# Routed experts placed in the slots of the second attention, and causal masks of 64 columns

## The chip, the cores and the metric

One core of a Trainium2 chip runs the whole program in one launch. The metric is the device time of that core in microseconds; the median of three runs of the kernel before is 3800.89 (3798.13 to 3801.47). 

## The reference

Two layers on x of 16 x 512 x 128 (f32): each adds an attention-like part and a feed-forward part of the normalised x to x. Only layer 1 is touched here.

```python
xn = layernorm(x)
x = x + causal_attention_twice(xn) + routed_experts(xn)
# attention: q, k, v = xn @ Wqkv.T + b   (16 heads of 8), causal softmax -> ctx
#   q2 = conv1d(ctx, 3 taps); ctx2 = causal softmax of q2 with the same k, v; out = ctx2 @ out_w.T + b
# experts (32 of them, each of 128 slots, top 8 of 32 per token):
oh = one_hot(flat_e); pos = (cumsum(oh, 0) * oh).sum(-1) - 1
buf = zeros(E, 128, H).at[flat_e, pos].set(flat_x, mode='drop')
gate, up = split(einsum('ech,efh->ecf', buf, gate_up_proj))
eo = einsum('ecf,ehf->ech', silu(gate) * up, down_proj)
out = sum over the 8 chosen of weight * eo[expert, pos]     # dropped where pos >= 128
```

The attention has two passes over the same keys and values for each of 16 batches, so 32 passes. An expert takes the first 128 tokens that chose it.

## The kernel before

The program runs in stages, each with instruction lists written out by hand for all five engines and its own semaphores, which are cleared after it: `learn` (a memory trained chunk by chunk), `attend0`, `mixture` (dense experts of layer 0, which also leaves the table of normalised rows with expert weights, the sum so far, and `chosen`, a 0/1 flag for each token and expert), then `routed` (L1989) and `layer1` (L2262).

`routed` works through 32 experts in 8 groups of 4 (Q = 4), in loops. For a group, `indices` finds the token of each slot: four matmuls with an upper triangle give running counts in each of 64 tiles of tokens (L2100), one more the counts of earlier tiles (L2104), DVE makes one-hot rows for the tile of each slot (L2208 to L2214), matmuls select the tile's counts (L2108, L2110), and DVE compares and sums to a row index (L2216 to L2225). `through` passes the group: POOL gathers 128 rows per expert by an indirect DMA (L2163), TensorE transposes them (L2116), multiplies by the gate and up weights (L2122), ACT and DVE gate, TensorE transposes (L2126) and multiplies by the down weights (L2130), DVE scales by the token's share (L2244), and POOL adds each expert's rows into the sum in memory by an indirect DMA that accumulates (L2175). Adds follow one another, each waiting for the last to land, since two experts may hold one token.

`layer1` uses the class `Attention` (L964). A turn is one pass over one batch; there are 32, firsts and seconds mixed (batch b's second comes at least three turns after its first), plus turns -2 and -1 that only prepare and turn 32 that only ends. From turn 3 on, odd turns are seconds, and so is turn 30. A turn has 16 slots: four groups g of four heads, and four key tiles t of 128. In slot (g, t), `tensor_scores` (L1164) makes transposed scores of keys of tile t against queries from tile t on: width 512, 384, 256, 128. In the same slot `tensor_maxima` (L1135) makes the scores of the next turn's batch for the row maxima, of the same widths. ACT takes the exponentials (L1261), DVE the maxima (L1303), and `tensor_values` (L1192) multiplies the probabilities of the slot before by the values, in f32 (L1203). In tiles 0 and 1 (wide slots) the heads come in two units, the second after the first; in tiles 2 and 3 (narrow slots) all four heads go together. f32 operands of the scores are split into three bf16 parts, laid into partitions in groups of 8 (PITCH): six are used (PARTS), rows 62 and 63 of each half carry the shift by the maximum, and the other rows are zero. The two halves of 64 partitions hold two heads and run side by side.

PSUM banks are handed out by two rings (L941): `m` of two double banks (maxima, shift, context, values, output) which DVE frees, and `s` of three banks (exponentials, projections, convolution, whole transposes) which ACT frees. `plan` (L1053) lists the jobs of both in the order in which TensorE issues them; a job waits until the job two (m) or three (s) before it is freed. Extra jobs sit at fixed slots: query and key projections of a first at slots 0 and 4, values at 8, convolution of a second in two halves at 4 and 8, the whole transposes at slot 3, context transposes at slots 1 and 9, output at slot 5 of the turn after a second. ACT, DVE and TensorE follow the same order.

POOL splits q and k of turn p + 2 into parts once ACT has written them (`pool_parts`, L1093), SP copies the parts into the rows of the query and key buffers (`sync_rows`, L1119), and the maxima of the next turn but one wait for that. The causal mask is added by matmuls on top: for each tile a pair of halves n = 0, 1 picks (`pick`) rows of `qmask` or `kmask` with 0 or -1e30. For the maxima their widths are 128 and 64 columns (L1155), for the scores 64 and 128 (L1188), two halves of partitions each:

```python
for n in range(2):
    for half in range(2):
        rows = slice(half * HALF, (half + 1) * HALF)
        last = nc.tensor.matmul(outs[half][:, k0:k0 + HALF + n * HALF], self.pick[n][rows, :], self.kmask[n][rows, :], start=False, stop=n == 1)
```

## Time and profile before

| what | value |
|---|---|
| median of runs | 3800.89 us |
| profiled execution | 3806.04 us, its span 3804.1 us |
| mean granted TensorE clock | 0.937 |
| busy shares | PE 87%, DVE 69%, ACT 54%, POOL 22% |
| `mixture` | to 2342 us |
| `routed` | 2351.64 to 2558.50 us |
| `layer1` | 2558.50 to 3804.1 us |

Times of rows are microseconds from the first instruction of the span; a line such as L1188 is that of the kernel's file. Both spans of the last two stages come from the profile's timeline. A busy share is a mean over stages that are limited in different ways, so the stages are read one by one. TensorE's matmuls overlap and their ends are modelled: the start of the next one tells how long one really held the engine.

### The profile page before, as it was taken

Reading aid. Unit: us, or ns where it says so; the run is one execution under the profiler, and the core shown is the slowest. Engines: PE = TensorE matmul, PEld = TensorE weight load, DVE = VectorE, ACT = ScalarE, POOL = GpSimd, SP = SyncE. Lnnn points to the kernel's source line nnn. Section 1 sums busy time; section 2 is a strip of 40 time slices with the busy share of each in tenths; the row PEclk is TensorE's granted clock in tenths of the full one; section 3 lists DMA queues with packets and bytes.
Section 4 is the critical chain, followed back from the end, with each engine's and each line's share of the span. In section 5 each row is a group of like instructions: output and inputs, shape, how many; then the busy total and the mean of one; then the engine's idle time right before and its main releaser. Section 6 shows DMA issues by size and latency. Waiting matters only on the chain. (4 is left out here: it accounts for less than half of the span.)

```text
span 3804.1 us, 77742 instructions
## 1 busy us (share of the span) xinstructions
PE 3308.0 (87%) x30322; PEld 1937.0 (51%) x30322; DVE 2613.1 (69%) x5296; ACT 2045.7 (54%) x4082; POOL 832.5 (22%) x744
## 2 busy tenths in 40 slices
PE   6787599999998899999999995336999999999998
PEld 6776222222222677777777773223555555555554
DVE  5776688888884476676767674326777777777774
ACT  5663177777777344443334441003666666666666
POOL 3321211111110332424233230442111111111100
PEclk8988699999999899999999997557999999999999
DMA  4100111111110100111101001222112111111100
GB/s 121 27 12 0 57 51 48 46 51 51 51 46 10 31 27 27 31 32 31 33 21 40 23 25 48 49 37 61 39 39 58 36 45 51 46 44 39 53 25 27
DMA packets 179534, 151.12 MB, mean 40 GB/s; under 512 B 44284, under 2 KB 159964, under 8 KB 178908
## 3 DMA queue, kind: packets, MB, share of 16 engines
q1 hardware_dynamic: 173020, 141.28, 12.9%
q0 software_dynamic: 6144, 4.72, 0.9%
q8 instruction: 255, 4.18, 0.5%
q14 instruction: 115, 0.94, 0.1%
HBM read 48.58 MB, written 32.65 MB: 21 GB/s over the span
## 5 line engine op out<-in xcount | busy, mean ns | idle before, releaser
L1303 DVE TENSOR_REDUCE b_maxima<-psum 128x2 f32<-128x1024 f32 (+3 forms) x768 | 780.3, 1045 | 272.1 <-PE psum L1155 270.6
L1261 ACT ACTIVATE b_prob<-psum 128x512 f32<-128x512 f32 (+2 forms) x1536 | 725.2, 525 | 357.6 <-PE psum L1188 342.8
L1303 DVE TENSOR_REDUCE c_maxima<-psum 128x2 f32<-128x1024 f32 x512 | 602.5, 1221 | 132.6 <-PE psum L1150 131.5
L1261 ACT ACTIVATE c_prob<-psum 128x512 f32<-128x512 f32 x1024 | 536.0, 601 | 187.3 <-PE psum L1181 187.3
L1765 PEld LDWEIGHTS psum<-consts_layer,a_hid 128*128 128x128 f32 x4096 | 476.2, 192 | 53.6 <-issue 53.3
L1765 PE MATMUL psum<-consts_layer,a_hid 128*128 128x128 f32 x4096 | 477.8, 274 | 0.0
L1755 PE MATMUL psum<-a_x1t,consts_layer 128*128 128x512 f32 x1024 | 460.4, 595 | 10.5 <-issue 10.2
L1822 ACT ACTIVATE a_hid<-psum,consts_layer 128x512 f32<-128x512 f32 x512 | 347.1, 687 | 203.8 <-PE psum L1755 197.3
L1181 PE MATMUL psum<-b_qa,b_ka 64*128 64x512 bf16 (+3 forms) x2048 | 367.9, 302 | 57.4 <-ACT b_prob L1261 57.1
L1203 PE MATMUL psum<-b_prob,b_v 128*32 128x512 f32 (+3 forms) x4096 | 384.7, 448 | 0.3 <-ACT b_prob L1261 0.2
L1150 PE MATMUL psum<-b_ka,b_qa 62*128 62x512 bf16 (+3 forms) x2048 | 301.9, 304 | 29.6 <-DMA b_ka<-b_part 21.8
L1181 PE MATMUL psum<-c_qa,c_ka 64*128 64x512 bf16 x1024 | 270.9, 381 | 63.3 <-ACT c_prob L1261 61.7
L1967 DVE SCALAR_TENSOR_TENSOR a_acc<-psum,a_gprob,a_acc 128x128 f32<-128x128 f32 x512 | 143.8, 343 | 263.1 <-PE psum L1765 246.6
L1755 PEld LDWEIGHTS psum<-a_x1t,consts_layer 128*128 128x128 f32 x1024 | 187.1, 191 | 211.9 <-issue 200.2
L1188 PE MATMUL psum<-b_kmask,b_pick 64*128 64x64 bf16 (+1 forms) x4096 | 277.9, 204 | 0.0
L1203 PE MATMUL psum<-c_prob,c_v 128*32 128x512 f32 x2048 | 272.8, 605 | 0.1
L1181 PEld LDWEIGHTS psum<-b_qa,b_ka 64*128 64x128 bf16 x2048 | 122.1, 93 | 285.8 <-ACT b_prob L1261 230.7
L1155 PE MATMUL psum<-b_qmask,b_pick 64*128 64x128 bf16 (+1 forms) x4096 | 245.0, 204 | 0.0
L1150 PE MATMUL psum<-c_ka,c_qa 62*128 62x512 bf16 x1024 | 202.6, 394 | 29.6 <-DMA c_ka<-c_part 16.6
L1155 PEld LDWEIGHTS psum<-b_qmask,b_pick 64*128 64x128 bf16 x4096 | 199.2, 96 | 50.4 <-issue 3.7
L1188 PEld LDWEIGHTS psum<-b_kmask,b_pick 64*128 64x128 bf16 x4096 | 192.0, 94 | 46.7 <-issue 0.5
L1851 POOL TENSOR_TENSOR a_share<-a_gprob,consts_layer 128x512 f32<-128x512 f32 x128 | 134.3, 1050 | 274.2 <-DVE a_gprob L1906 265.4
(326 smaller groups left out, 4302.1 us busy)
## 6 DMA issues: line engine op xcount, KB each, us to landing
b_qa<-b_part SPq DMA_DIRECT2D x192, 128.0 KB, 2.4
c_qa<-c_part SPq DMA_DIRECT2D x96, 128.0 KB, 2.5
c_ka<-c_part SPq DMA_DIRECT2D x96, 128.0 KB, 2.5
b_ka<-b_part SPq DMA_DIRECT2D x96, 128.0 KB, 2.4
consts_layer<-layer_in SPq DMA_DIRECT2D x1, 5419.0 KB, 19.2
m_xin<-x SPq DMA_DIRECT2D x16, 256.0 KB, 3.8
xnt<-m_xt SPq DMA_DIRECT2D x16, 256.0 KB, 2.7
c_xt<-xnt SPq DMA_DIRECT2D x16, 256.0 KB, 2.7
```

The costliest lines, as they stand in the source:

```text
L1150: last = nc.tensor.matmul(out[:, half, k0:k0 + w], qa[rows, hh, t * P:(t + 1) * P], ka[rows, hh, 0:w], start=True, stop=not self.causal)
L1155: last = nc.tensor.matmul(out[:, half, k0 + t * P + n * HALF:k0 + w], self.pick[n][rows, :], self.qmask[n][rows, :], start=False, stop=n == 1)
L1181: last = nc.tensor.matmul(outs[half][:, k0:k0 + w], ka[rows, hh, t * P:(t + 1) * P], qa[rows, hh, q0:S], start=True, stop=not self.causal)
L1188: last = nc.tensor.matmul(outs[half][:, k0:k0 + HALF + n * HALF], self.pick[n][rows, :], self.kmask[n][rows, :], start=False, stop=n == 1)
L1203: last = nc.tensor.matmul(self.acc[32 * j:32 * (j + 1), q0:S], self.values(p)[:, t, column:column + 32], self.prob[:, s % 2, j, q0:S], sta ...
L1261: self.nc.scalar.activation(out, src, ACT.Exp, scale=SCALE).then_inc(self.s.free, 1)
L1303: self.nc.vector.reduce_max(out, src, X).then_inc(self.m.free, 1)
L1755: nc.tensor.matmul(bank[4 + u % 3], K("up0", e * F0 + f * P, P), x1t[n][:, :], start=True, stop=True).then_inc(up_ready.sem, 1)
L1765: last = nc.tensor.matmul(tiled(2 + e % 2)[:, t, :], hid[:, e % 2, f, t * P:(t + 1) * P], K("down0", (e * FC + f) * D, D), start=f == 0, s ...
L1822: nc.scalar.activation(hid[:, e % 2, f, :], bank[4 + u % 3], ACT.Relu, bias=K("upb0", u, 1)).then_inc(hid_ready.sem, 1)
L1851: own.done(nc.gpsimd.tensor_tensor(share[k % 2][:, :, :], along(gprob[n][:, :, k], D), over(K("downb0", k * D, D), T), ALU.mult))
L1967: last = nc.vector.scalar_tensor_tensor(acc[n][:, t, :], tiled(2 + e % 2)[:, t, :], gprob[n][:, t, e:e + 1], acc[n][:, t, :], ALU.mult, AL ...
```

## The change

The stage `routed` goes. Its work becomes jobs of the second attention's slots, in a class `Routed`. Group g is found in turn g - 1 (the counts at slot 2, the selection at slot 4, indices by DVE at slots 2 and 4, then the gather on POOL) and passed in the turn after that (row transposes at slot 1, gate and up weights in two jobs at slots 5 and 6, gating by DVE at slot 7, transposes at slot 9, down weights at slot 11, then the four adds on POOL). So finding takes place in turns -1 to 6, passing in turns 0 to 7. All jobs but the selection use ring s; the selection uses ring m. The totals of all 32 experts and their sums over earlier tiles are made once in turn -2, by 32 matmuls of one column. The counts are now one matmul of 512 columns (earlier tiles) and four of 128 added onto it in PSUM. ACT now copies the counts, the up result and the scaled output. SP issues a group's expert weights in its finding turn.

A batch's output may use the sum only when all adds are done, so the outputs of batches 0 to 2 are parked in three buffers by a copy on DVE and finished by POOL in turns 9, 11 and 13; the others go as before, from turn 10 on.

The causal mask's fully hidden block (queries 0 to 63 against keys 64 to 127 of a tile) no longer comes from the mask matmuls: the seventh row of each group of eight, zero before, holds an indicator for each tile, 1 on the query side and -2^80 on the key side. It is written once into all seven buffers, by POOL and seven DMAs in the setup. The mask matmuls keep the two triangles of 64 columns.

```diff
-               ("out1", D), ("outb1", D), ("pick", 2 * D), ("qmask", D + D // 2), ("kmask", D + D // 2), ("upto", D), ("before", NT),
+               ("out1", D), ("outb1", D), ("pick", 2 * D), ("qmask", HALF), ("kmask", HALF), ("tiles", T), ("upto", D), ("before", NT),
...
+            nc.gpsimd.memset(self.cover[:, :, :, :], 0.0).then_inc(self.covers_ready, 1)
+            pool.wait_ge(self.covers_ready, 1)
+            nc.gpsimd.memset(self.cover[:, 0, :, 0:HALF], 1.0)
+            nc.gpsimd.memset(self.cover[:, 1, :, HALF:P], COVER).then_inc(self.covers_ready, 1)
+            pool.wait_ge(self.covers_ready, 2)
+            own_tile = self.K("tiles")[0:P // PITCH, :].unsqueeze(2).broadcast_to([P // PITCH, T, P])
+            for w in range(2):
+                nc.gpsimd.tensor_tensor(self.covers[:, w], self.cover[:, w], own_tile, ALU.mult).then_inc(self.covers_ready, 1)
...
+        if self.causal:
+            sp.wait_ge(self.covers_ready, 4)
+            for w, rows in enumerate((self.qa, self.ka)):
+                for x in rows:
+                    sp.dma_start(x[PARTS::PITCH, :, :], self.covers[:, w].rearrange("r t p -> r (t p)").unsqueeze(1).broadcast_to([P // PITCH, H // 2, S])
+                                 ).then_inc(self.covers_loaded, 16)
...
-                        last = nc.tensor.matmul(out[:, half, k0 + t * P + n * HALF:k0 + w], self.pick[n][rows, :], self.qmask[n][rows, :], start=False, stop=n == 1)
+                        k1 = k0 + t * P + n * HALF
+                        last = nc.tensor.matmul(out[:, half, k1:k1 + HALF], self.pick[n][rows, :], self.qmask[rows, :], start=False, stop=n == 1)
...
-                        last = nc.tensor.matmul(outs[half][:, k0:k0 + HALF + n * HALF], self.pick[n][rows, :], self.kmask[n][rows, :], start=False, stop=n == 1)
+                        last = nc.tensor.matmul(outs[half][:, k0 + n * HALF:k0 + (n + 1) * HALF], self.pick[n][rows, :], self.kmask[rows, :], start=False, stop=n == 1)
...
-def routed(nc, ctx0, K, ps, bank, chosen, gate_up, down, table_d, sum_d):
...
+class Routed:
...
+    LOCAL, SELECT, ROWS, UP, GATE, HIDDEN, DOWN = 2, 4, 1, (5, 6), 7, 9, 11
+    TOTAL, BEFORE, UPTO = 1, 2, 3
...
+    def jobs_m(self, p, s):
+        g = self.finding(p)
+        return [("sel", g)] if g is not None and s == self.SELECT else []
+    def tensor_s(self, pe, p, s):
...
+            if job[0] == "total":
+                pe.wait_ge(self.tables_ready, 1)
+                for e in range(E1):
+                    last = nc.tensor.matmul(out[0:NT, e:e + 1], self.chosen[:, e, :], self.ones[:, :], start=True, stop=True)
...
+            if job[0] == "local":
+                g = job[1]
+                total = self.total[:, g * Q:(g + 1) * Q].unsqueeze(2).broadcast_to([P, Q, P])
+                nc.tensor.matmul(out[0:NT, :], self.earlier[:, :], total, start=True, stop=False)
+                for q in range(Q):
+                    last = nc.tensor.matmul(out[0:NT, q * P:(q + 1) * P], self.chosen[:, g * Q + q, :], self.upto[:, :], start=False, stop=q == Q - 1)
...
+            if job[0] == "gu":
+                g, j = job[1:]
+                if j == 0:
+                    pe.wait_ge(ring.free, ring.count("rt", g))
+                    pe.wait_ge(self.loaded[g % 2], 32 * (g // 2 + 1))
+                for q in range(2):
+                    last = nc.tensor.matmul(out[:, q * 2 * F1:(q + 1) * 2 * F1], self.rt[:, (2 * j + q) * P:(2 * j + q + 1) * P],
+                                            self.wgu[g % 2][:, 2 * j + q, :], start=True, stop=True)
...
+    def tensor_m(self, pe, p, s):
...
+            pe.wait_ge(self.hot_ready, g + 1)
+            pe.wait_ge(self.att.s.free, self.att.s.count("local", g))
+            for q in range(Q):
+                nc.tensor.matmul(out[:, 0, q * P:(q + 1) * P], self.onehot[:, q, :], self.count[:, q * P:(q + 1) * P], start=True, stop=True)
+            for q in range(Q):
+                last = nc.tensor.matmul(out[:, 1, q:q + 1], self.passed[:, q, :], self.ones[0:NT, :], start=True, stop=True)
...
+    def scalar(self, act, p, s):
...
+            if job[0] == "gu":
+                both = src[:, 0:4 * F1].rearrange("p (q x) -> p q x", q=2)
+                pair = slice(2 * job[2], 2 * job[2] + 2)
+                nc.scalar.activation(self.th[:, pair, :], both[:, :, 0:F1], ACT.Tanh, scale=0.5)
+                last = nc.scalar.activation(self.gu[:, pair, :], both, ACT.Copy)
...
+            if job[0] == "eo":
+                g = job[1]
+                if g >= 2:
+                    act.wait_ge(self.added, 16 * Q * (g - 1))
+                for q in range(Q):
+                    last = nc.scalar.activation(self.out[g % 2][:, q, :], src[:, q * D:(q + 1) * D], ACT.Copy,
+                                                scale=self.row[g % 2][:, q, D + g * Q + q:D + g * Q + q + 1])
...
+    def vector(self, dve, p, s, own):
...
+        g = self.finding(p)
+        if g is not None and s == self.LOCAL:
+            group = slice(g * Q, (g + 1) * Q)
...
+            nc.vector.tensor_tensor(self.passed[:, :, :], slots, self.incl[:, group].unsqueeze(2).broadcast_to([NT, Q, CAP]), ALU.is_ge)
+            own.done(nc.vector.tensor_tensor(self.onehot[:, :, :], slots, self.excl[:, group].unsqueeze(2).broadcast_to([NT, Q, CAP]), ALU.is_ge))
+            nc.vector.tensor_tensor(self.onehot[:, :, :], self.onehot[:, :, :], self.passed[:, :, :], ALU.subtract).then_inc(self.hot_ready, 1)
+        if g is not None and s == self.SELECT:
+            src = m_ring.bank("sel", g)
+            dve.wait_ge(m_ring.ready, m_ring.count("sel", g))
+            nc.vector.tensor_scalar(self.tiles[:, :], src[:, 1, 0:Q], float(P), None, ALU.mult)
+            nc.vector.tensor_scalar(self.below[:, :, :], src[:, 0, :].rearrange("p (q k) -> p q k", q=Q), self.K("slot"), None, ALU.is_le
+                                    ).then_inc(m_ring.free, 1)
+            dve.wait_ge(m_ring.free, m_ring.count("sel", g))
+            own.done(nc.vector.tensor_reduce(self.slot[:, :], self.below[:, :, :], X, ALU.add))
+            own.done(nc.vector.tensor_tensor(self.slot[:, :], self.tiles[:, :], self.slot[:, :], ALU.add))
+            nc.vector.tensor_scalar(self.index[:, g * Q:(g + 1) * Q], self.slot[:, :], self.K("spare"), None, ALU.min).then_inc(self.index_ready, 1)
...
+    def pool_gather(self, pool, p):
+        g = self.finding(p)
+        if g is None:
+            return
+        pool.wait_ge(self.index_ready, g + 1)
+        if g >= 2:
+            pool.wait_ge(self.att.s.free, self.att.s.count("eo", g - 2))
+        self.hold(pool)
+        for q in range(Q):
+            self.nc.gpsimd.indirect_dma_start(out=self.row[g % 2][:, q, :], out_offset=None, in_=self.table_d,
+                                              in_offset=bass.IndirectOffsetOnAxis(ap=self.index[:, g * Q + q:g * Q + q + 1], axis=0)
+                                              ).then_inc(self.gathered[g % 2], 16)
+    def pool_add(self, pool, p):
+        g = self.passing(p)
+        if g is None:
+            return
+        pool.wait_ge(self.att.s.free, self.att.s.count("eo", g))
+        for q in range(Q):
+            e = g * Q + q
+            if e:
+                pool.wait_ge(self.added, 16 * e)
+            self.hold(pool)
+            self.nc.gpsimd.indirect_dma_start(out=self.sum_d, out_offset=bass.IndirectOffsetOnAxis(ap=self.index[:, e:e + 1], axis=0),
+                                              in_=self.out[g % 2][:, q, :], in_offset=None, compute_op=ALU.add
+                                              ).then_inc(self.added, 16)
+    def sync_weights(self, sp, p):
+        g = self.finding(p)
+        if g is None:
+            return
+        if g >= 2:
+            sp.wait_ge(self.att.s.ready, self.att.s.count("eo", g - 2))
+        sp.dma_start(self.wgu[g % 2][:, :, :], self.gate_up[:, g * Q:(g + 1) * Q, :]).then_inc(self.loaded[g % 2], 16)
+        sp.dma_start(self.wdn[g % 2][:, :, :], self.down[:, g * Q:(g + 1) * Q, :]).then_inc(self.loaded[g % 2], 16)
+FIRST_GROUP = -1
+PARKED = 3
...
+        routed = Routed(ctx, ctx0, nc, K, att, FIRST_GROUP, chosen, gate_up, down, table_d, sum_d)
+        whole_turn = FIRST_GROUP + GROUPS + 1
+        outputs = {}
...
+            if b < PARKED:
+                p = whole_turn + 1 - whole_turn % 2 + 2 * b
...
+                    routed.sync_weights(sp, p)
+                    if p in outputs:
+                        i, b = order.index(p), outputs[p].batch
+                        if i == 0:
+                            sp.wait_ge(routed.added, 16 * E1)
+                        elif outputs[order[i - 1]].parked:
+                            sp.wait_ge(res_stored, 16 * i)
+                        else:
+                            sp.wait_ge(att.m.free, att.m.count("out", outputs[order[i - 1]].batch))
                         sp.dma_start(before[:, :, :], sum_d[b * S:(b + 1) * S, :].rearrange("(t p) d -> p t d", p=P)
...
+                        if outputs[p].parked:
+                            pool.wait_ge(biased, i + 1)
+                            pool.wait_ge(att.m.free, att.m.count("out", b))
+                            nc.gpsimd.tensor_tensor(before[:, :, :], before[:, :, :], park[b][:, :, :], ALU.add).then_inc(unparked, 1)
+                    if second(p + 2):
+                        routed.pool_gather(pool, p)
                     if att.has(p + 2):
                         att.pool_parts(pool, p + 2, att.s.count(*(("k", p + 2) if first(p + 2) else ("q", p + 2, 1))))
+                    if not second(p + 2):
+                        routed.pool_gather(pool, p)
+                    routed.pool_add(pool, p)
...
+                        src = tiled(att.m.bank("out", b)[:, 0, :])
                         dve.wait_ge(att.m.ready, att.m.count("out", b))
...
+                        if b < PARKED:
+                            nc.vector.tensor_copy(park[b][:, :, :], src).then_inc(att.m.free, 1)
+                        else:
+                            i = order.index(p)
+                            dve.wait_ge(biased, i + 1)
+                            dve.wait_ge(res_stored, 16 * i)
+                            nc.vector.tensor_tensor(res[:, :, :], src, before[:, :, :], ALU.add).then_inc(att.m.free, 1)
+                    routed.vector(dve, p, s, own)
...
-                routed(nc, sems, K, ps, bank, chosen, gate_up, down, table_d, sum_d)
-                sems.clear(nc)
-            with Semaphores() as sems:
-                layer1(nc, sems, K, ps, bank, xnt2_d, sum_d, result)
+                layer1(nc, sems, K, ps, bank, chosen, gate_up, down, xnt2_d, table_d, sum_d, result)
...
-    put("qmask", hidden[half])
-    put("qmask", hidden[half + HALF][:, HALF:], P)
+    put("tiles", (p[:, None] % PITCH == np.arange(T)[None, :]).astype(np.float32))
+    put("qmask", hidden[half][:, 0:HALF])
     put("kmask", hidden.T[half][:, 0:HALF])
```

## Rows read from the trace of the kernel before

**Rows 1.** Length, busy us of PE, PEld, DVE, ACT, POOL; clock, DMA share, GB/s.

```profile
2351.64:2558.50 206.86, 70.81 (x304) 54.80 (x304) 73.00 (x297) 13.45 (x24) 89.97 (x107) 0.52 0.24 46
...
2587.73:2618.40 30.67, 22.98 (x211) 11.69 (x211) 24.43 (x27) 1.38 (x2) 6.33 (x4) 0.56 0.23 68
2618.40:3759.40 1141.00, 1085.65 (x16765) 577.86 (x16763) 852.79 (x1020) 775.08 (x1639) 163.32 (x134) 1.00 0.15 43
```

**Rows 2.** Timeline at the edges of the routed stage: start, length, work.

```profile
2351.64 0.34 SPq L2077 DMA_DIRECT2D r_wgu<-gate_up  x1
...
2547.92 1.55 POOL L2175 DMA_INDIRECT sum<-r_out,r_index  x1 [0.16 <-issue]
2558.50 0.82 SPq L2328 DMA_DIRECT2D b_xt<-xnt  x2
```

**Rows 3.** Chain of waits within the second attention, by line.

```profile
by line: PE psum L1203 27.8%; PE psum L1181 13.8%; ACT b_prob L1261 12.0%; PE psum L1150 10.1%; PE psum L1188 9.8%; PE psum L1155 5.8%; PE psum L2387 4.3%; issue 4.1%; PE psum L1212 3.2%; PE psum L1220 1.6%; PE psum L2378 1.4%; PE psum L240
```

**Rows 4.** Timeline of PE, slots 12 to 15 of a turn, without extra jobs.

```profile
3384.11 0.39 PE L1181 MATMUL psum<-b_qa,b_ka 64*128 64x512 bf16 x2
...
3385.34 0.39 PE L1181 MATMUL psum<-b_qa,b_ka 64*128 64x512 bf16 x1 [0.23 <-ACT b_prob L1261]
...
3389.29 0.27 PE L1181 MATMUL psum<-b_qa,b_ka 64*128 64x256 bf16 x2
...
3390.95 0.23 PE L1181 MATMUL psum<-b_qa,b_ka 64*128 64x128 bf16 x2
...
3391.24 0.22 PE L1150 MATMUL psum<-b_ka,b_qa 62*128 62x128 bf16 x2
...
3392.20 0.39 PE L1181 MATMUL psum<-b_qa,b_ka 64*128 64x512 bf16 x2
```

**Rows 5.** Same view, two turns: slots 0, 4, 8 and two extra jobs.

```profile
3354.56 0.39 PE L1181 MATMUL psum<-b_qa,b_ka 64*128 64x512 bf16 x2
...
3364.71 0.39 PE L1181 MATMUL psum<-b_qa,b_ka 64*128 64x512 bf16 x2
...
3369.17 1.16 PE L2404 MATMUL psum<-consts_layer,b_ctxt 128*128 128x128 f32 x8
...
3374.43 0.39 PE L1181 MATMUL psum<-b_qa,b_ka 64*128 64x512 bf16 x2
...
3401.59 0.39 PE L1181 MATMUL psum<-b_qa,b_ka 64*128 64x512 bf16 x2
3402.30 1.56 PE L2387 MATMUL psum<-b_cpad,consts_layer 128*128 128x256 f32 x6
...
3410.49 0.39 PE L1181 MATMUL psum<-b_qa,b_ka 64*128 64x512 bf16 x2
...
3428.40 0.39 PE L1181 MATMUL psum<-b_qa,b_ka 64*128 64x512 bf16 x2
```

**Rows 6.** Timeline of SP at the start of the second attention.

```profile
2573.70 4.48 SPq L1116 DMA_DIRECT2D b_ka<-b_one  x8
...
2585.33 0.60 SPq L1124 DMA_DIRECT2D b_ka<-b_part  x1
```

**Rows 7.** Timeline of POOL: an add; first and last of a turn's parts.

```profile
2544.26 1.55 POOL L2175 DMA_INDIRECT sum<-r_out,r_index  x1 [0.15 <-POOL r_still L2156]
...
3367.33 1.04 POOL L1101 CAST b_part<-b_qk 128x1024 bf16<-128x1024 f32 x1 [4.51 <-ACT b_qk L2435]
...
3371.76 2.13 POOL L1107 TENSOR_TENSOR b_part<-b_rest,b_part 128x1024 bf16<-128x1024 f32 x1
```

**Rows 8.** Groups by line and form, second attention: count, busy us, mean ns.

```profile
L1303 DVE TENSOR_REDUCE b_maxima<-psum 128x2 f32<-128x1024 f32 x244 | 299.1, 1226 | 161.0 <-PE psum L1155 159.6
```

**Rows 9.** The same view of the routed stage.

```profile
L2122 PE MATMUL psum<-r_wgu,r_rt 128*128 128x192 f32 x64 | 23.4, 547 | 5.7 <-ACT r_rt L2139 5.7
...
L2116 PE MATMUL psum<-consts_shared,r_row 128*128 128x128 f32 x32 | 8.9, 434 | 3.0 <-DMA r_row<-table,r_index 3.0
...
L2217 DVE TENSOR_SCALAR r_below<-psum,consts_layer 128x512 f32<-128x512 f32 x8 | 6.0, 750 | 0.3
```

More of the change, by code:

```diff
@@ L162 @@
 PITCH = 8
-HALF = P // 2
 SHIFT = HALF - 2
@@ new lines, in __init__ @@
+        self.ones = sb("ones", [P, 1], BF16)
+        self.total = sb("total", [P, E1], BF16)
+        self.excl = sb("excl", [NT, E1])
+        self.incl = sb("incl", [NT, E1])
+        self.count = sb("count", [NT, Q * P], BF16)
+        self.passed = sb("passed", [NT, Q, CAP], BF16)
+        self.onehot = sb("onehot", [NT, Q, CAP], BF16)
+        self.tiles = sb("tiles", [P, Q])
+        self.below = sb("below", [P, Q, P])
+        self.slot = sb("slot", [P, Q])
+        self.index = sb("index", [P, E1], I32)
@@ new lines, in passing, with jobs_s @@
+    def passing(self, p):
+        return self.finding(p - 1)
+    def jobs_s(self, p, s):
+        jobs, g, h = [], self.finding(p), self.passing(p)
+        if p == -2 and s == self.TOTAL:
+            jobs.append(("total",))
+        if p == -2 and s == self.BEFORE:
+            jobs.append(("excl",))
+        if g is not None and s == self.LOCAL:
+            jobs.append(("local", g))
+        if h is not None:
+            if s == self.ROWS:
+                jobs.append(("rt", h))
+            if s in self.UP:
+                jobs.append(("gu", h, self.UP.index(s)))
+            if s == self.HIDDEN:
+                jobs.append(("ht", h))
+            if s == self.DOWN:
+                jobs.append(("eo", h))
+        return jobs
@@ new lines, in pool_setup, with hold @@
+    def pool_setup(self, pool):
+        nc = self.nc
+        nc.gpsimd.tensor_copy(self.upto[:, :], self.K("upto"))
+        nc.gpsimd.tensor_copy(self.earlier[:, :], self.K("before"))
+        nc.gpsimd.memset(self.still[:, :], 0.0)
+        nc.gpsimd.memset(self.total[:, :], 0.0)
+        nc.gpsimd.memset(self.ones[:, :], 1.0).then_inc(self.tables_ready, 1)
+        pool.wait_ge(self.tables_ready, 1)
+    def hold(self, pool):
+        if self.holds:
+            pool.wait_ge(self.held, self.holds)
+        self.holds += 1
+        self.nc.gpsimd.tensor_tensor(self.still[:, 0:1], self.still[:, 1:2], self.still[:, 1:2], ALU.add).then_inc(self.held, 1)
```

389 lines of the change are left out of this document (137 added, 252 removed).

## The prediction

> **What bounds the kernel now.** I read the busy time by stretches first, then the timeline at the stage edges, then the chain of waits inside the second attention, then single slots of it. Times are of the profiled execution: it took 3806.04 us with a span of 3804.1, and the median of the timed runs is 3800.89, so 5.15 us come off at the end.
>
> The routed stage is a chain, not a load. In its 206.86 us no engine is busy over 90, TensorE has only 70.8 and that at clock 0.52, which is the 1.2 GHz level [rows 1]. It stands alone between 2351.64, where its first weight load is issued, and 2558.50, where the attention's first load is issued [rows 2]. That is 25.9 us for each of eight groups, most of it one step waiting for the other.
>
> The second attention runs at clock 1.00 from 2618.40 to 3759.40; DVE is 75% busy, ACT 68%, TensorE reads 95%, but its matmul ends are modelled [rows 1]. The reader should see from the chain that TensorE sets the pace: its lines make up some 80% there, ACT's exponentials 12%, and the two mask lines (L1188, L1155) 15.6% together [rows 3]. Four slots without extra jobs last 3392.20 - 3384.11 = 8.09 us: 5.18 for the two wide ones, 1.66, 1.25 [rows 4]. The turns repeat: an even one lasts 3392.20 - 3354.56 = 37.64, an odd one 3428.40 - 3392.20 = 36.20 [rows 4, 5].
>
> **Stage removed.** 206.9 us, both clears and the idle at its edges included [rows 2]. The next thing late is the attention's own setup, which takes its old length and more. The constants shrink by 252 of their columns, worth at most half a microsecond: nothing.
>
> **Setup: +7 us.** SP waits for DVE's seven memsets, issues eight loads in 4.48 us from 2573.70, and then twelve row loads, the last at 2585.33 [rows 6], so 0.65 us apart; TensorE starts the maxima when it has landed, 2.4 us later at 2587.73 [rows 1]. The change puts seven loads of 128 KB, the row loads' size, ahead and waits for all: 7 x 0.65 + 2.4 = 6.9. POOL gets a memset of 1024 columns, two of 256 and two products of 512; at its 1.04 for a conversion and 2.13 for a subtraction of 1024 columns [rows 7] that is 1.0 + 0.5 + 2.1, with the waits between them some 4.5 us ahead of the value memsets, so its first parts end about 5 us later; SP's own delay covers that. The 32 one-column matmuls and two copies of turn -2 fall under the same cover. Bounds 3 (the loads' landing overlaps) and 14 (POOL's and SP's delays add).
>
> **Masks: -46 us.** Every pair of mask matmuls shrinks from 192 columns to 128. Twelve matmuls of a narrow slot (2 x 320 columns counted once for both halves) start within 3391.24 - 3390.95 = 0.29 us [rows 4], 0.45 ns a column; so 64 columns are 0.029, and the two halves run side by side. In four slots there are 16 such groups. In the two narrow slots TensorE never waits, so all eight count. In the two wide ones the chain goes scores, exponential, scores of the second half: TensorE waits at 3385.34 for ACT [rows 4], and the first maxima of each lie in that wait, so six count. 14 x 0.027 (64 columns at 2.4 GHz) = 0.38 us of 8.09, 1.5 a turn, and 31 turns give 47; the last turn is ACT's, the slots with context transposes are nearer DVE's limit: 46. Bounds: 32 x 64 groups x 0.027 = 55 above; 20 if more than half is eaten where DVE becomes the slower side: two wide maxima are 2 x 1.23 = 2.45 us [rows 8] of the 2.6 a wide slot lasts. The indicator rows cost nothing: the contraction is 62 rows wide either way.
>
> A rule speaks against this. The trace's narrow slot has 12 matmuls, each with its own weight load, in 0.29 us, 24 ns each [rows 4]. The Trainium skill (TensorE: Matmul & The Clock Gate, "Back-to-back issue gap") gives about 81 ns for each load-and-matmul pair of 128 columns, so loads and not columns would set the pace and narrowing would bring nothing; the trace disagrees threefold. By the rule the term would be 0 and the time 46 us higher.
>
> **Routed jobs within the turns: +45.5 us.** First what such jobs cost now. Slots 4 to 7 with the convolution, 1.56 us on TensorE, last 3410.49 - 3401.59 = 8.90, so 0.81 over 8.09. With the key projection and the output, whose matmuls are 1.16, they last 3374.43 - 3364.71 = 9.72, so 1.63 over. Slots 0 to 3 of the odd turn, with context and whole transposes, are 9.39, 1.30 over [rows 4, 5]. So a job in a wide even slot is half hidden behind ACT, and elsewhere it costs its matmuls and about 0.05 to 0.1 us for the switch.
>
> Per group, from the routed stage at half clock, halved: the up projection 23.4 / 8 / 2 = 1.46, two jobs, so 1.65 with switches; the row transposes 8.9 / 8 / 2 = 0.56, so 0.6, and as much for the hidden ones [rows 9]; the down projection is the shape of the output's 8 matmuls, 1.08 [rows 5]. That is 3.93 for passing, in turns 0 to 7: 31.5. Finding: the counts are 1024 bf16 columns at 0.45 ns and a switch, 0.52; the selection 512 columns and four one-column matmuls, half hidden, 0.25.
>
> What DVE adds: about 1.6 us at slot 2, hidden, since DVE has two narrow slots to catch up. At slot 4 it waits for the selection and then does two passes of 512 columns (0.75 each [rows 9]) and three small ones, 2.2 us, between the two wide maxima. Behind it stands the second maximum of slot 4, then those of slot 5; TensorE has two banks of lead and by my count of slot 5 meets them 1.2 us early. Finding is thus 0.52 + 0.25 + 1.2 = 2.0, in turns 0 to 6: 14. Sum 45.5. In turn -1, 30.67 us of which DVE is busy 24.4 [rows 1], the same work of group 0 costs 3.5 (0 to 5).
>
> Bounds of the 45.5: 32 if DVE never stalls TensorE and two jobs hide; 72 if all 5 us of DVE's work in a group go on top (7 x (5 - 1.2) = 27 more). ACT gains ten passes over 3200 columns, at that same 0.75 for 512 some 4.7 us a group; it is busy 68% [rows 1] and its passes fall into slots that TensorE's part of the job has lengthened: hidden.
>
> POOL: an add takes 3.66 us to the next (2544.26 to 2547.92), the parts of a first turn 3371.76 + 2.13 - 3367.33 = 6.6 [rows 2, 7]. Slot 8 begins 19.9 us into an even turn [rows 5], so slot 11 at some 28, and 32 with the new jobs; four adds end 47 us in, 5 or 6 us into the next turn, and the parts cannot start before its slot 4, at 10. Hidden. SP's weight loads wait for nothing that is not past. Parking replaces a DVE add by a copy of the same 512 columns and gives POOL three more additions on an idle engine: 0.
>
> **Sum.** 3806.0 - 206.9 + 6.9 - 46 + 45.5 + 3.5 = 3609.0; less 5.15 is 3604.
>
> **Rivals.** (A) DVE becomes the bound in the shared turns. For: it stands at 75% already and in slot 4 has 2.45 + 2.2 us of work in a slot of some 3.7 [rows 8, 9]. Against: the narrow slots leave it 0.9 us each. Price 27: 3631. Chance 0.2. (B) The masks bring nothing, because loads or the slower side of DVE and ACT set the pace. For: the rule and the 12% of ACT in the chain [rows 3]. Against: the narrow slots' even 0.45 ns a column. 3604 + 46 = 3650. Chance 0.08. (C) More hides than I count: routed jobs 32, masks 50: 3604 - 13.5 - 4 = 3586. For: half-hidden jobs now [rows 5]. Chance 0.15. (D) Slower: POOL's adds, beside the row transfers on the same DMA engines, take longer. Their place is POOL's queue ahead of the parts of turn p + 2; from slot 11 of one turn to slot 4 of the next there are about 19 to 21 us, of which four adds take 14.6. Each add over 5.3 us then lengthens a turn by four times the excess, and the kernel is slower from 200 / 8 = 25 us a turn, 11.5 us an add. At 12 us: 3604 + 8 x 27 = 3820. Against: 3.66 now, with DMA share 0.24 there and 0.15 in the attention [rows 1]. Chance 0.02. (E) The work isn't hidden at all but only moved, each group keeping its 25.9 us: the engines would stand still 8 x 25.9 = 207 less the 45.5 counted: 3765. Against: each step has slots between it and the next. Chance 0.02. My forecast 0.53.
>
> **Range.** The forecast and A, C and most of what lies between: 3582 to 3648. Two measurements of this kernel are told apart from 0.2%, 7.6 us, on; faster 0.97, same 0.01, slower 0.02.
>
> **What would show it.** A span of about 3607. The attention begins near 2351. First maxima 36 us after it, not 29. Turns past 8 at 36.1 and 34.7, not 37.64 and 36.20; four plain slots 7.71. Shared turns near 42 and 41. TensorE's new waits at the maxima of slot 5, on DVE; if they are nowhere, C; if in every slot, A. If the narrow slots still last 1.25, the mask step is wrong. POOL's parts must still be released by ACT and not by adds.

## The result, and the profile after

The changed kernel took 3637.82 us (median of four, 3637.05 to 3640.65) beside 3800.81 for the kernel before: ratio 0.9574, 95% interval 0.9557 to 0.9590, so faster by 4.3%. The forecast was 3604 with a range of 3582 to 3648: the sign and the range held, the point was 34 too low. Beside the kernel before on another chip the same kernel took 3620.09, ratio 0.952 (0.9504 to 0.9536); experiment 3 is about that difference.

The profiled execution of the first comparison, by stages as in [rows 1]: setup up to the first maxima, turn -1, the eight turns with routed jobs (0 to 7), turns 8 to 30, the last turn and the end. Columns: length, busy us of PE, PEld, DVE, ACT, POOL, then granted clock, DMA share, GB/s.

```profile
2351.64:2393.29 41.65, 10.34 (x52) 7.08 (x52) 12.07 (x10) 1.75 (x4) 18.00 (x21) 0.54 0.43 87
2393.29:2426.69 33.40, 22.35 (x218) 12.02 (x218) 30.10 (x35) 1.96 (x3) 10.57 (x9) 0.55 0.33 78
2426.69:2779.79 353.10, 322.44 (x4590) 177.01 (x4592) 259.71 (x334) 228.79 (x509) 120.65 (x127) 0.96 0.26 56
2779.79:3596.24 816.45, 770.91 (x12459) 404.40 (x12455) 628.37 (x758) 574.56 (x1218) 131.00 (x109) 1.00 0.17 46
3596.24:3635.90 39.66, 29.27 (x359) 13.45 (x358) 4.28 (x10) 25.19 (x53) 2.56 (x2) 1.00 0.10 28
```

The stage of 206.86 us [rows 1] is gone; the second attention begins at 2350.1, as early as the routed stage did. Turns 8 to 30 average 35.5, at full clock throughout. The eight shared turns average 44.1 and are the only stretch of the main part whose clock is below 1.00. A slot chain without extra jobs, slots 12 to 15 of turn 10 (the answer to [rows 4]):

```profile
2879.01 0.39 PE L1201 MATMUL psum<-b_qa,b_ka 64*128 64x512 bf16 x2
...
2884.03 0.27 PE L1201 MATMUL psum<-b_qa,b_ka 64*128 64x256 bf16 x2
...
2885.59 0.23 PE L1201 MATMUL psum<-b_qa,b_ka 64*128 64x128 bf16 x2
...
2886.73 0.39 PE L1201 MATMUL psum<-b_qa,b_ka 64*128 64x512 bf16 x2
```

That is 7.72 us where it was 8.09: the 7.71 that was forecast. The two narrow slots, 1.66 and 1.25 before, last 1.56 and 1.14.

I divide each profile at instants that any kernel here has: the first instruction of the attention stage, DVE's first maxima, the first exponential of turn 0, and those of turns 8 and 31. From here on a slot or turn, too, runs from its first exponential on ACT to the next one's. Column 3 is the setup, column 4 turn -1. "Unedited" is the changed kernel once more; the chip of the first runs is not on record. In us ("routed jobs" are turns 0 to 7 less the 282.5 of the kernel with masks alone):

```
kernel               chip  first maxima  to first exp  turns 0-7  routed jobs  turns 8-30  rest
before                     30.0          29.9          293.6                   847.4       44.7
changed (1st)              43.2          33.4          353.1      70.6         816.4       39.7
masks_alone          2     43.0          29.2          282.5                   816.5       44.4
changed, unedited    2     43.2          33.5          329.5      47.0         816.5       42.7
gather_first (1st)   2     43.1          36.7          325.5      43.0         816.5       44.1
gather_first_again   2     43.2          36.9          324.4      41.9         816.4       42.6
plain_rows           2     43.2          33.2          332.3      49.8         816.4       43.3
no_adds              2     43.2          32.8          332.0      49.5         816.5       40.6
select_late          2     43.2          32.0          314.6      32.1         816.4       43.2
changed, unedited    14    43.1          33.5          352.0      69.5         816.4       44.1
parts_last           14    43.1          38.0          344.1      61.6         816.5       41.2
setup_split          14    31.9          32.6          351.0      68.5         816.5       43.7
parts_setup          14    31.9          37.2          344.6      62.1         816.5       42.0
select_late_setup    10    32.0          31.0          314.8      32.3         816.5       43.7
```

Two things vary that no edit explains. The "rest" is 39.7 at a granted clock of 1.00 in the first profile after and 40.6 to 44.4 at 0.84 to 0.96 in the runs behind it, 44.7 at 0.88 before: 5 us of the first comparison that the change didn't earn. And the attention stage, which the table counts from its start, starts between 2346.9 and 2355.3 in the changed kernels, at 2350.3 and 2346.9 in two profiles of one kernel on chip 2. So medians a few us apart are read together with the stretches that an edit touches. The last turn of the kernel before:

```profile
3759.48:3804.10 44.62, 34.63 (x359) 14.92 (x358) 4.29 (x10) 25.19 (x53) 2.54 (x2) 0.88 0.08 25
```

### The profile page after: what moved, and what is told of

The parts are those of the page before. It is cut to its first block and busy times, and to the rows that moved or that the text cites. A ratio compares the mean times of both kernels' runs of the same rounds, so it can differ in the third digit from the quotient of the medians.

```text
span 3635.9 us, 77371 instructions
## 1 busy us (share of the span) xinstructions
PE 3242.8 (89%) x30347; PEld 1888.3 (52%) x30347; DVE 2579.5 (71%) x5080; ACT 2060.6 (57%) x4148; POOL 838.3 (23%) x752
## 5 line engine op out<-in xcount | busy, mean ns | idle before, releaser
L1208 PE MATMUL psum<-b_kmask,b_pick 64*128 64x64 bf16 x4096 | 251.8, 190 | 0.0
L1175 PE MATMUL psum<-b_qmask,b_pick 64*128 64x64 bf16 x4096 | 220.9, 190 | 1.4 <-issue 1.4
L1208 PEld LDWEIGHTS psum<-b_kmask,b_pick 64*128 64x128 bf16 x4096 | 184.4, 95 | 46.8 <-issue 1.2
L1169 PEld LDWEIGHTS psum<-b_ka,b_qa 62*128 62x128 bf16 x2048 | 106.3, 94 | 186.2 <-DVE b_maxima L1323 70.1
```

The costliest lines, as they stand in the source:

```text
L1169: last = nc.tensor.matmul(out[:, half, k0:k0 + w], qa[rows, hh, t * P:(t + 1) * P], ka[rows, hh, 0:w], start=True, stop=not self.causal)
L1175: last = nc.tensor.matmul(out[:, half, k1:k1 + HALF], self.pick[n][rows, :], self.qmask[rows, :], start=False, stop=n == 1)
L1208: last = nc.tensor.matmul(outs[half][:, k0 + n * HALF:k0 + (n + 1) * HALF], self.pick[n][rows, :], self.kmask[rows, :], start=False, stop= ...
```

## The experiments

The traces left two suspects for the 25 us too many in the shared turns. The first stands in turn 2 of the changed kernel. DVE's steps of the selection, and POOL's first two passes for the parts:

```profile
2529.97 1.03 POOL L1113 CAST b_part<-b_qk 128x1024 bf16<-128x1024 f32 x1 [7.76 <-ACT b_qk L2499]
...
2530.75 0.69 DVE L2210 TENSOR_REDUCE r_slot<-r_below 128x4 f32<-128x512 f32 x1
...
2531.09 2.13 POOL L1115 TENSOR_TENSOR b_rest<-b_qk,b_part 128x1024 f32<-128x1024 f32 x1
...
2531.47 1.77 DVE L2211 TENSOR_TENSOR r_slot<-r_tiles,r_slot 128x4 f32<-128x4 f32 x1
...
2533.28 1.07 DVE L2212 TENSOR_SCALAR r_index<-r_slot,consts_layer 128x4 int32<-128x4 f32 x1
2533.28 1.04 POOL L1117 CAST b_part<-b_rest 128x1024 bf16<-128x1024 f32 x1
2534.26 4.07 DVE L1323 TENSOR_REDUCE b_maxima<-psum 128x2 f32<-128x1024 f32 x4
...
2535.53 0.34 PE L1169 MATMUL psum<-b_ka,b_qa 62*128 62x384 bf16 x2 [2.19 <-DVE b_maxima L1323]
```

A step over four elements takes 1.77 us and ends within 0.02 us of POOL's subtraction; the next, as small, takes 1.07 and ends with POOL's conversion. TensorE then waits 2.19 for the maxima. The same two steps take 1.77 and 1.07 on chip 2 as well. (POOL's parts are released by ACT, as forecast.) The second suspect was in the odd turns. There POOL gathers first and no DVE step is stretched, and yet all engines wait in slot 6 at full clock: experiment 3.

**1. Masks alone.** The kernel before with the masks and covers (the indicator rows and their loads) of the change only: of its diff the hunks of the masks, the covers and the constants, none of the routed stage or of the output.

> The kernel before with only the masks of the change: seven cover loads in the setup, mask matmuls of 64 columns, the routed stage left where it was. Theory: the masks and the setup behave as predicted, 1.35 us off each of 31 turns (the turns past 8 of the changed kernel last 36.31 and 34.83 against 37.64 and 36.20), 5 off the last turn, 7 more in the setup: 3801 - 42 - 5 + 7 = 3761. Rival: the gain of the later turns comes in part from another place (output parked, code that lies differently), then 3775 or more. If the setup costs more than 7, it shows as a later first exponential.

3774.77, ratio 0.9917 (0.9900 to 0.9933), 30 below the 3804.88 beside it. Turns 0 to 30 give back 293.6 + 847.4 - 282.5 - 816.5 = 42.0, the 42 of the theory, and turns 8 to 30 are the changed kernel's to 0.1 us, so parking the output adds nothing there. The time misses the 3761 expected and meets the rival's 3775, but not for the rival's reason: the setup costs 13.0, not 7, the last turn gives nothing (its 5 us were the clock), and the kernel before took 4 more on this chip. SP's queue in this kernel:

```profile
2574.72 2.07 SPq L1130 DMA_DIRECT2D b_qa<-b_covers  x3
2576.84 5.87 SPq L1130 DMA_DIRECT2D b_ka<-b_covers  x4
2586.78 4.69 SPq L1135 DMA_DIRECT2D b_ka<-b_one  x8
```

The seven covers take 8.0 us to issue, the last four 1.47 each, and then SP waits 4.1 for their landing: 12.1 from the first cover to the first of the ones.

**2. The gather first in every turn.**

```diff
-                    if second(p + 2):
-                        routed.pool_gather(pool, p)
+                    routed.pool_gather(pool, p)
                     if att.has(p + 2):
                         att.pool_parts(pool, p + 2, ...)
-                    if not second(p + 2):
-                        routed.pool_gather(pool, p)
```

> The changed kernel with POOL's gather ahead of the parts in every turn, not only in half of them. Theory 1: in even turns POOL's passes over 1024 columns hold up DVE's two tiny steps of the selection (1.77 and 1.07 us where they take 0.16 and 0.23 elsewhere), TensorE then waits 2.2 us for the maxima and its clock falls. With POOL waiting for the index before its parts this goes: even shared turns 47.3 to 44 or less, odd ones unchanged near 41.5 to 43, four even turns, 3638 - 14 = 3624, range 3615 to 3630. Theory 2 (the gather itself freezes the other engines and the parts have no share): within 3 us of 3638. Rival: parts later by the gather's 5 us make the row transfers late: above 3640.

3617.40 in the first group of runs, whose odd turns were 39.09; the text below on experiment 3 says why that comparison misled. Run again beside the unedited changed kernel:

> The kernel with the gather ahead of the parts in every turn, run again. On a chip with the freeze: odd turns 41.5, even ones 43 to 46, some 2 us below the changed kernel beside it for each of four even turns, 5 to 10 in all. On one without it: 3617 as before and the changed kernel at about 3625.

3613.30 against 3620.09: 7 us (ratios to before 0.9502, 0.9486 to 0.9518, and 0.9520, 0.9504 to 0.9536). Of these the edit can claim about 2: in the two profiles turns 0 to 7 are 5.1 shorter and turn -1 is 3.4 longer, and 3.3 us lie ahead of the attention, where the kernels are the same. The selection is now quick (0.16 and 0.23 us) and slot 5 is 3.18 in turns 0 and 2, but the parts have moved beside the gate, and the same thing happens there (turn 2 of the first run):

```profile
2531.76 1.29 DVE L2218 SCALAR_TENSOR_TENSOR r_th<-r_th,r_gu 128x384 f32<-128x384 f32 x1
2532.71 2.33 POOL L1115 TENSOR_TENSOR b_rest<-b_qk,b_part 128x1024 f32<-128x1024 f32 x1
2533.09 2.37 DVE L2219 TENSOR_TENSOR r_h<-r_th,r_gu 128x384 f32<-128x384 f32 x1
```

The gate's product takes 0.56 elsewhere. It ends 0.42 us behind POOL's subtraction, and POOL's next pass, which starts beside it, takes 1.25 instead of 1.04. Turn -1 loses its 3.4 us because the parts of turn 1 end later, SP loads their rows first and the shift rows of turn 0 stand behind them in its queue.

**3. What the odd turns wait for.** Two kernels that each leave out one kind of indirect transfer: the gathers, with plain loads on SP in their place (the experts then work on the wrong rows), and the adds (the experts' outputs are then missing from the sum).

```diff
-                        routed.pool_gather(pool, p)          # on POOL, four indirect
+                    routed.sync_plain_rows(sp, p)            # on SP, four plain, after the same waits
```

```diff
             self.hold(pool)
-            self.nc.gpsimd.indirect_dma_start(out=self.sum_d, ..., compute_op=ALU.add).then_inc(self.added, 16)
+            pool.sem_inc(self.added, 16)
```

> The changed kernel with the indirect gather left out: SP loads the first 512 rows of the table by plain transfers of the same size into the same tile, after the same wait for the index. The experts so work on the wrong rows. Theory 2: four indirect transfers back to back on POOL freeze TensorE, DVE and ACT (their semaphore updates come 2 to 4.5 us late, at granted clock 1.00 too), 2 to 3 us in each of eight turns and in turn -1: 3638 - 9 x 2.5 = 3615; odd shared turns 42 to 40. Rival (late updates are TensorE's own work at the lower clock, or DVE's load): odd turns stay at 41.4 to 43 and the time within 5 us of 3638.

> The changed kernel with the indirect adds left out, POOL only counts the semaphore up: the experts' outputs are missing from the sum. The slot in which the adds of a group begin (13) lasts 3.3 us in shared turns where it lasts 2.69 in later ones. Theory: a single indirect transfer at a time costs the others only that 0.6 us a turn, 8 x 0.6 = 5: 3633. Rival: adds cost nothing and slot 13 is long for another reason: within 2 us of 3638. Rival: adds take DMA engines from the row transfers: more than 10 us.

3618.45 and 3619.27 (0.9505 and 0.951, intervals 0.0016 to each side): odd turns 39.09 in both, and in experiment 2 as well. The first lies near the 3615 of the theory of the gather, the second far below its 3633. Three unlike edits with one effect are suspect, so the unedited kernel went along with the next groups.

> The changed kernel, nothing edited, beside the next three on one chip. Three edits that have nothing in common (another order in even turns, no indirect gather, no adds) each brought the odd shared turns from 41.4 to 39.09. Either each of them removes the freeze of 2 to 3 us at a gather, or the freeze belongs to the chip or to the one execution and not to the kernel. In the first case odd turns are again 41.4 to 43, ratio to before 0.957; in the second they are 39.09 here, even ones near 43 to 46, and the ratio is about 0.953.

> The changed kernel, nothing edited, once more beside the next two. The kernels of the first group of runs (chip 2) had odd shared turns of 39.09 and no late updates at a gather, those of the second (chip 14), the changed kernel among them, 41.5 to 43. If the freeze belongs to the chip, this kernel and the next show the same odd turns: both 39.09 or both above 41. If the order of POOL's work made it, this one has 41.4 to 43 and the next 39.09.

On chip 14 it took 3641.92 (0.9573) and had the delay, on chip 2 3620.09 and had none. The kernel before took 3803.8 and 3802.9 beside them. On chip 2 turns 0 to 7 take 332.3 us without gathers, 332.0 without adds and 329.5 with both, so there neither transfer costs anything, and the delay belongs to the chip or its state: chip 2 ran two groups without it, chip 14 one with it. Slots 5 and 6 of turn 3, first the changed kernel's first profile, then chip 2:

```profile
2578.42:2582.71 4.29, 4.29 (x58) 2.61 (x54) 3.77 (x6) 2.35 (x7) 2.45 (x4) 1.00 0.07 19
2582.71:2586.18 3.47, 2.41 (x41) 1.01 (x40) 0.66 (x1) 1.68 (x5) 1.61 (x2) 1.00 0.29 71
```

```profile
2564.02:2567.21 3.19, 3.19 (x46) 1.76 (x44) 3.12 (x6) 2.35 (x6) 1.65 (x3) 1.00 0.04 10
2567.21:2569.63 2.42, 2.42 (x48) 1.50 (x44) 1.79 (x2) 1.80 (x4) 1.81 (x3) 1.00 0.22 55
```

The same work takes 7.76 and 5.61 us at clock 1.00; in slot 6 of the first, TensorE is busy 2.41 of 3.47, DVE 0.66, ACT 1.68: nobody is the bound. The table of waits has a releaser there that the profile can't place, in the first profile and in those of chip 14, and in none of chip 2's or chip 10's (changed kernel, first profile, 2430 to 2740; us waited, times, longest wait):

```profile
DVE b_maxima L1323 <- remote: 23.7, 7, 4.6
ACT b_prob L1281 <- remote: 18.2, 4, 9.2
```

These 11 waits all end 5.7 to 6.2 us after the first transfer of a gather starts. Slot 13, shortly after the first add of a group starts, is 3.2 to 3.4 in seven of the eight turns of the first profile, and 2.69 on chip 2. The kernel before has no such wait in its attention, where no indirect transfer runs. What they are I can't say: no kernel without gathers or adds ran on a chip with the delay.

**4. The parts later still.** The gather first, and in even turns the parts behind the gate.

```diff
+                    if first(p + 2) and routed.passing(p) is not None:
+                        pool.wait_ge(routed.h_ready, routed.passing(p) + 1)
```

> The changed kernel with the gather first in every turn and, in even shared turns, POOL's parts held until DVE has made the hidden values (slot 7), so that they run beside no DVE step that has both inputs and its output in SBUF. Theory 1: with the gather first alone the collision only moved, to the gate's second product (2.37 us where it takes 0.55 alone) and slots 8 and 9 (5.26 and 4.93 against 3.24 and 3.66). Now even turns go to the odd ones' 39.1 plus their own share of 1.5 (output) or 0.4: 39.5, 39.5, 40.6, 40.6. Sum of turns 0 to 7 is 3 x 39.09 + 37.95 + 160.2 = 315.4 against 325.5 with the gather first alone, so 10 us below that: ratio 0.948. Rival: the parts still land late or collide with another step (the values of slot 8): no gain over the gather first, 0.9504.

3637.65, 0.9566 (0.9550 to 0.9582), on chip 14. Of the 7.9 us that turns 0 to 7 gain against the unedited kernel there, 4.5 go back in turn -1, as in experiment 2. The time is only 4.3 below the unedited kernel, where 10 below the gather first alone was expected. The expected ratio, 0.948, was made from chip 2's runs, but the chip accounts for only 0.005 of the miss of 0.009. The rival, no gain over the gather first, is nearer, though the gather first alone didn't run on this chip. A reason shows in slot 15 of the even turns, which is 2.8 to 3.3 where it is 1.2; that held parts make the rows late there is my reading, and no run tests it.

**5. The selection at slot 6.** One number: `SELECT` 4 becomes 6. The parts of an even turn are over by then, and the gate follows them.

> The changed kernel with the selection at slot 6 instead of slot 4, its order of POOL's work kept. By then POOL's parts of an even turn, which last 6.6 us from the middle of slot 4, are over, so neither the selection's small steps nor the gate run beside them. Theory 1: slot 5 of even turns falls from 5.44 to 3.1 (11.8 to 4.2 where it has the output too), slot 6 grows from 2.4 to 2.9; even turns 40 to 41 without a freeze, 42 to 43.5 with it; 15 to 20 us below the changed kernel beside it. Rival: DVE has no room in slots 6 and 7 (1.4 of maxima, 2.0 of selection and 1.1 of gate in 3.6 us) and the stall moves to slot 8: less than 8 us below.

3601.23, 0.9464 (0.9448 to 0.9480), 18.9 below the unedited kernel beside it; 14.9 of it are turns 0 to 7 and 1.5 turn -1. DVE in turn 2:

```profile
2524.42 0.15 DVE L2206 TENSOR_SCALAR r_tiles<-psum 128x4 f32<-128x4 f32 x1
2524.49 0.74 DVE L2207 TENSOR_SCALAR r_below<-psum,consts_layer 128x512 f32<-128x512 f32 x1
2525.27 0.69 DVE L2210 TENSOR_REDUCE r_slot<-r_below 128x4 f32<-128x512 f32 x1
2525.99 0.16 DVE L2211 TENSOR_TENSOR r_slot<-r_tiles,r_slot 128x4 f32<-128x4 f32 x1
2526.18 0.23 DVE L2212 TENSOR_SCALAR r_index<-r_slot,consts_layer 128x4 int32<-128x4 f32 x1
2526.32 0.69 DVE L1323 TENSOR_REDUCE b_maxima<-psum 128x4 f32<-128x512 f32 x1
2526.92 0.55 DVE L2218 SCALAR_TENSOR_TENSOR r_th<-r_th,r_gu 128x384 f32<-128x384 f32 x1
2527.51 0.56 DVE L2219 TENSOR_TENSOR r_h<-r_th,r_gu 128x384 f32<-128x384 f32 x1
```

No step is stretched. DVE does selection and gate back to back, and still slot 6 is 2.71, slot 7 1.19 and slot 8 3.32: the stall did not move. Turns 0 to 6 are 39.22, 39.07, 39.34, 39.07, 40.42, 39.07, 40.42, where the unedited kernel beside it has 41.67, 39.09, 42.75, 39.09, 44.96, 39.09, 44.90. The clock of turns 2, 4 and 6 is 1.00 where it was 0.96. The gather moves with the selection, but on this chip it costs nothing (experiment 3). On a chip with the delay the late selection wasn't run.

**6. The setup in two parts.** SP loads covers, ones and rows of turn 0's two buffers, and only then the other five covers and six ones.

```diff
-                att.sync_setup(sp)
+                att.sync_setup(sp, 0)    # qa[0], ka[0]
 ...
                         att.sync_rows(sp, p + 2)
+                    if p == -2:
+                        att.sync_setup(sp, 1)    # the rest; turn 1's maxima wait for it
```

> The changed kernel with SP's setup in two parts: covers, ones and row loads of the first turn's two buffers first, the other five covers and six ones behind them. The cover loads are not 0.65 us each but 1.15, and in the kernel with masks alone the first maxima come 43.0 us after the stage's first load where they came 30.0 before. Theory (SP's queue sets the start): five covers and six ones fewer ahead, 5 x 1.15 + 6 x 0.58 = 9 us earlier: 9 off the changed kernel's time beside it. Rival: DVE's memsets or the landing of the rows set it, or turn -1 waits for the rows of turn 1 instead: 0 to 4.

> Both of these together. The two touch different stretches, so they add: the gain of the parts last plus 9 us, ratio about 0.9455. Rival: less than the sum if turn -1 or turn 0 waits for the rows that are now loaded later.

3630.84 against 3641.92 beside it, 11.1 less (0.9545, 0.9529 to 0.9561), and 3623.96 against 3637.65, 13.7 less: first maxima at 31.9 instead of 43.1. SP's queue did set the start (9 us were expected). The two edits add within what the medians can tell; 0.953 misses the 0.9455 expected because the parts' gain isn't there.

**7. Both improvements.**

> The selection at slot 6 and the setup in two parts together. Theory: they add, since one touches turns 0 to 6 and the other the 43 us ahead of the first maxima: 12 us below the kernel with the late selection alone on a chip without the freeze (3601 - 12 = 3589, ratio 0.9432), odd turns 39.07, even ones 39.3 and 40.4, first maxima 32 us after the stage's first load. On a chip with the freeze every shared turn is 2 to 3 us longer, except that the even ones no longer have a collision: 3607 to 3612, ratio 0.948 to 0.950. Rival: turn -1 waits for what is now loaded later, then half of the 12 comes back between the first maxima and the first exponential (over 34 us).

3594.04, 0.9446 (0.9433 to 0.9459), the best here, on chip 10, where this kernel shows no delay. First maxima 32.0, first exponential 31.0 later, turns 0 to 7 314.8: the parts of the two edits stand side by side, and the attention stage is 11.4 shorter than with the late selection alone, as forecast (12). The median is 7.2 below that kernel's, and 5 above the expected 3589; the stage starts 1.9 later in this profile, and the rest of the difference isn't explained.

## Why the prediction came out as it did

Against the forecast's span of 3607.1 the first profile's 3635.9 is 28.8 over. The other 5 of the 34 are the 5.15 that I subtracted because the profiled run before lay above its median; the one after did not. By steps:

- **Stage removed:** right. The attention starts 1.5 us earlier still, less than that start varies between runs.
- **Setup:** mis-sized, +6.3. Forecast 6.9 at 0.65 a load and 2.4 of landing, by the row loads [rows 6]; the covers took 8.0 to issue and 4.1 to land. The bound of 14 held it. I priced a load by its bytes. What makes the covers slower than rows of the same size isn't shown.
- **Turn -1:** +3.5 forecast, 33.4 - 29.9 = 3.5 measured; against masks alone it is 4.2.
- **Masks:** 42.0 of 46, from the kernel with masks alone. The plain slots came out (7.72 for 7.71), but 1.5 a turn took all sixteen slots as plain ones; measured are 1.33 (even) and 1.37 (odd). Rival B is out: the narrow slots fell from 1.25 to 1.14 and from 1.66 to 1.56. The Trainium skill's 81 ns a pair (TensorE: Matmul & The Clock Gate, "Back-to-back issue gap") are not what these loads of 64 rows cost: 12 of them with their matmuls start within 0.29 us, 24 ns each [rows 4].
- **Routed jobs:** 45.5 forecast, 70.6 in the first profile, 47.0 on chip 2. The agreement on chip 2 is luck: 47.0 is 32.1 for the jobs, the lower bound of the forecast and all that is left with the selection at slot 6, and 14.9 for the collision, which no step had. Passing costs 37.95 - 34.83 = 3.12 in turn 7, not 3.93, since slots 1, 5, 6, 9 and 11 grow by 0.38, 0.39, 0.85, 0.38 and 1.10 where I had 0.6, 1.65 for the two, 0.6 and 1.08; finding costs 39.09 - 37.95 = 1.14, not 2.0, because slot 5 has no stall in an odd turn (3.19, and 3.08 in turn 7, where nothing is found). The stall that I expected in slot 5 is there in even turns alone, 14.9 us in four turns, and from another cause: POOL's passes stretch two tiny DVE steps by 2.5 us, TensorE idles, and the clock of turns 2, 4 and 6 is 0.96 on chip 2, where the late selection has 1.00.
- **The delay on some chips,** 22.5 us (352.0 against 329.5; 353.1 in the first profile): no step of mine had it, and no row of the trace of before shows it.
- **Last turn:** -5.0, clock.

Of the 46 for the masks 12 belong to turns 0 to 7 and 34 to the rest, where 847.4 - 816.4 = 31.0 came: +3.0. The sum is -1.5 + 6.3 + 26.0 + 3.0 - 5.0 = 28.8; the 26.0 are turns 0 to 7, 353.1 against 293.6 - 12 + 45.5 = 327.1. That the range held this time is in part luck: its upper part stood there for DVE's load, and the collision and the delay filled it.

**The rivals.** A gave nearly the right time (3631) for a reason that is false: the late selection keeps every DVE step and its turns cost 32.1, so DVE's load was never the bound. C had the right size for the jobs (32), not for the masks (50, measured 42), and the wrong sum, since the setup, the collision and the delay lay outside it. D and E are out: POOL's parts waited for ACT and not for adds, which start 3.8 us apart on average where D needs over 5.3, and a group costs 4 us with the late selection, not 25.9.

**What I should have seen.** [rows 7] showed POOL passes of 1.04 and 2.13 us, and the diff put DVE steps with two SBUF inputs at the slot where they start. In the routed stage POOL had no such long pass, only indirect transfers and steps over one column, and the gate's two steps read one input from PSUM, where they now read both from SBUF; so their short times there were no price for this place. The Trainium skill (SBUF — State Buffer, "SBUF: two separate sides") states the rule: VectorE and GpSimd share one port pair as an exclusive lock, held for a whole instruction, and the DVE operations concerned are those in a two-port mode and, against a GpSimd operation that reads SBUF, those with two SBUF inputs. The traces agree: 1.77 for 0.16, 1.07 for 0.23 and 2.37 for 0.56, the first two ending with POOL's pass, while L2210, with one SBUF input, keeps its 0.69 beside POOL's conversion. L2212 has one tensor input too; that it is in a two-port mode no row shows.

## What to carry to other kernels

When work moves from a stage of its own between the slots of another, price each small step by what runs beside it there: ask of every DVE step with two SBUF inputs whether a long POOL pass can be under way, and choose the slot by that before choosing it by load. Here one number, 4 to 6, was worth 19 us of the time, 15 of them in the shared turns. Count an added wait in a setup by the queue behind it and split it so that only what the first turn needs stands ahead. And run the unedited kernel beside the edited ones: the first group here would have credited three edits with a difference that the unedited kernel shows too, between two chips. Set a difference in medians beside the stretches that the edit can't touch: of the 7 us of experiment 2 some 3 lay there.

## What the chip showed unexpectedly

- Four-element DVE steps took 1.77 and 1.07 us beside POOL's passes; 0.16 and 0.23 otherwise.
- One kernel took 3641.9 us on chip 14 and 3620.1 on chip 2, the kernel before 3803.8 and 3802.9. The 22.5 us in the shared turns go with waits of up to 4.6 us at DVE that the profile can't place and that end 5.7 to 6.2 us after a gather starts, in odd turns at clock 1.00 too. Whether it is the chip or its state in that group of runs, and why, is open.
- In the last turn, where TensorE has gaps, the changed kernel had clock 1.00, 0.92 and 0.88 in three profiles and took 39.7, 42.7 and 44.1 us.
- Cover loads of 128 KB were issued 0.69 us apart at first and 1.47 later, where row loads of that size take 0.65.
